# Down projection of a dequantised feed-forward layer: the fourth block of output columns goes from pre-scaled weights to integer weights with a running sum on VectorE

## The reference, cut to what matters

```python
x = x + tanh(g_xattn) * xattn(layernorm(x), ctx, ctx, ...)     # 32 batches, 64 channels, 512 columns
x = x + tanh(g_ffn) * ffn(layernorm(x), ...)

def dequant(qweight, scales, zeros):                # 4-bit words, groups of 128 rows
    return q * s[g] - (z[g] + 1) * s[g]             # = (q - (z + 1)) * s[g],  g = k // 128

def ffn(x2):                                        # x2: 2048 rows x 512
    gate, up = x2 @ Wg, x2 @ Wu                     # 512 -> 1376
    inter = gate * sigmoid(gate) * up
    return (inter @ Wd).astype(float16)             # 1376 -> 512, Wd dequantised
```

## Time and profile before

| what | value |
|---|---|
| median of three runs | 733.96 us |
| profiled execution, its own time | 733.95 us |
| its span, first to last instruction | 732.1 us |
| PE busy | 681.9 us (93%), 4995 matmuls |
| DVE busy | 585.6 us (80%), 774 instructions |
| ACT busy | 475.4 us (65%), 841 |
| POOL busy | 350.9 us (48%), 455 |
| mean granted TensorE clock | 0.991 |
| chain that ended last | PE 63%, DVE 10%, ACT 8%, issue 7%, POOL 5%, DMA 5% |

### The profile page before, as it was taken

One profiled execution on the slowest core, in us unless ns is written; L12 is line 12 of the kernel. 1 busy time (PEld: TensorE's weight loads), 2 busy tenths in 40 slices (PEclk: granted clock), 3 DMA queues, 4 the chain that ended last, 5 costly groups with the idle time before them and its releaser, 6 DMA issues.

```text
span 732.1 us, 14401 instructions
## 1 busy us (share of the span) xinstructions
PE 681.9 (93%) x4995; PEld 352.8 (48%) x4995; DVE 585.6 (80%) x774; ACT 475.4 (65%) x841; POOL 350.9 (48%) x455
## 2 busy tenths in 40 slices
PE   5789999999999999999999996999999999999995
PEld 4444554455455545545554542445444444454443
DVE  6567888888888888788888567889988888888885
ACT  4856786677668667767775746567655665665562
POOL 6312212222221322222234663788777867886783
PEclk9999999999999999999999999999999999999998
DMA  4112312330332122112200100000000001000101
GB/s 108 32 37 64 89 46 54 92 90 10 88 89 63 33 77 73 34 49 74 76 6 24 25 6 2 1 0 2 1 29 30 1 0 44 15 1 16 43 1 58
DMA packets 30509, 28.96 MB, mean 40 GB/s; under 512 B 20047, under 2 KB 20186, under 8 KB 30466
## 3 DMA queue, kind: packets, MB, share of 16 engines
q1 hardware_dynamic: 28058, 27.73, 14.0%
q10 hardware_dynamic: 2408, 0.70, 0.4%
HBM read 22.42 MB, written 4.23 MB: 36 GB/s over the span
## 4 chain that ended last, share of the span: by engine, by line
PE 63%; DVE 10%; ACT 8%; issue 7%; POOL 5%; DMA 5%; SPq 1%; DVEq 0%; ACTq 0%; POOLq 0%
PE small L1025 8%; PE small L996 7%; PE pair L982 6%; PE pair L1226 5%; PE pair L1227 4%; DVE acc L1529 4%; PE small L1012 4%; PE pair L1250 4%; DMA rn_rows<-rn_parts 3%; POOL rn_sq L433 3%; PE pair L961 3%; ACT eq L664 3%; PE pair L1262 3%; PE small L1062 3%; PE small L1226 2%
## 5 line engine op out<-in xcount | busy, mean ns | idle before, releaser
L1529 DVE SCALAR_TENSOR_TENSOR acc<-pair,scale_T,acc 128x512 f32<-128x512 f32 (+1 forms) x176 | 131.8, 749 | 27.2 <-ACT acc L782 14.7
L1442 DVE TENSOR_TENSOR eq<-eq,pair 128x1024 f32<-128x1024 f32 x64 | 78.1, 1221 | 54.0 <-PE pair L1079 53.9
L565 POOL TENSOR_TENSOR yT<-yT,y_scaled 128x512 f32<-128x512 f32 (+1 forms) x78 | 100.3, 1287 | 19.6 <-ACT y_scaled L813 18.6
L1226 PE MATMUL pair<-ek,w_gu 128*128 128x512 f16 (+1 forms) x235 | 91.8, 391 | 2.8 <-DVE acc L1529 1.8
L655 ACT ACTIVATE ek<-pair,kneg 128x512 f32<-128x512 f32 x128 | 86.7, 686 | 10.3 <-DVE kneg L1437 10.1
L1227 PE MATMUL pair<-ekT,w_gu 128*128 128x512 f16 (+1 forms) x235 | 89.5, 381 | 0.0
L1434 DVE TENSOR_REDUCE qmax<-pair 128x16 f32<-128x1024 f32 x64 | 77.7, 1214 | 8.1 <-PE pair L961 8.1
L1250 PE MATMUL pair<-in_hi,d_int 128*128 128x512 f32 (+1 forms) x132 | 73.4, 559 | 10.9 <-DVE yT L1572 10.8
L664 ACT ACTIVATE eq<-pair 128x1024 f32<-128x1024 f32 x64 | 65.6, 1025 | 22.6 <-PE pair L1101 22.3
L1437 DVE TENSOR_REDUCE kneg<-pair 128x2 f32<-128x1024 f32 x64 | 77.9, 1218 | 0.6 <-PE pair L982 0.2
L1529 DVE SCALAR_TENSOR_TENSOR acc<-small,scale_T,acc 128x512 f32<-128x512 f32 (+1 forms) x88 | 65.9, 749 | 13.1 <-ACT acc L782 6.5
(11 more groups left out here) (187 smaller groups left out, 1434.4 us busy)
## 6 DMA issues: line engine op xcount, KB each, us to landing
xall<-in_x SPq DMA_DIRECT2D x16, 256.0 KB, 2.6
ctx_raw<-in_ctx SPq DMA_DIRECT2D x16, 256.0 KB, 2.8
out_x<-xall SPq DMA_DIRECT2D x16, 256.0 KB, 2.0
zero<-zeros_plus SPq DMA_DIRECT2D x8, 344.0 KB, 5.5
packed<-in_L_ffn_gate_qweight SPq DMA_DIRECT2D x4, 688.0 KB
packed<-in_L_ffn_up_qweight SPq DMA_DIRECT2D x4, 688.0 KB
packed<-in_L_ffn_down_qweight SPq DMA_DIRECT2D x10, 256.0 KB
zero<-zeros_plus SPq DMA_DIRECT2D x5, 256.0 KB, 5.0
```

Of the source, the lines that this page charges most:

```text
L565: pool.tensor_tensor(yT16[:, nt, :] if it == IT - 1 else total, total, y_scaled[:, nt, :], ALU.add).then_inc(z_add, 1)
L1226: pe.matmul(gu_bank[count % 3][0:w, :], lhsT, xT_hi[:, g, rows], start=True, stop=False)
L1442: dve.tensor_tensor(e, e, dve_pair[:, :, :], ALU.mult).then_inc(q_norm, 1)
L1529: dve.scalar_tensor_tensor(out=acc[0:w, n % 2, m, :], in0=gu_bank[(8 * n + job) % 3][0:w, :], scalar=scale_T[0:w, it, 4 * m + g:4 * m + g ...
```

## The change

All four blocks of output columns use the integer weights `d_int`. Block 3 gets two matmuls per unit in a bank that is started anew for each unit, and a second sum on VectorE, `add_sum(n, 3)`, placed directly behind `add_sum(n, 2)`. TensorE's next `high_product` of block 3 waits for it. The semaphore `z_dve` now counts two per unit. `plain_scaled`, `plain_high`, `plain_low`, `plain_sum`, their tiles and the DMA for `d_scale` are gone. `rows_transposed` takes the blocks in the order 0, 2, 1, 3.

```diff
@@ sync @@
-            sp.dma_start(d_scale[:, :, :], matrices[2][1][:, PLAIN].partition_broadcast(P)).then_inc(d_scale_in, 16)
@@ gpsimd @@
             ffn_normalised(7)
-            plain_scaled()
@@ scalar @@
                     step(PAIRS + 1, PAIRS // 2, 1, False, False, True, drain=True)
-                    plain_high()
                     ffn_normalised(8)
                     ffn_normalised(9)
                 scaled(n - 2, 1)
-                if n > IT and n % IT == 1:
-                    plain_sum(n // IT - 1)
@@ tensor: high_product, low_product, rows_transposed @@
-                elif n and nt == 2:
-                    pe.wait_ge(z_dve, n)
+                elif n and nt >= 2:
+                    pe.wait_ge(z_dve, 2 * n + nt - 3)
...
-                elif it == 0 and j:
-                    pe.wait_ge(y_plain, j)
-                if nt == NJ - 1:
-                    if n == 0:
-                        pe.wait_ge(d_lo, 2)
-                    pe.matmul(z_bank[nt], wd_hi[0:w, it, :], in_hi[0:w, n % 2, :], start=it == 0, stop=False)
-                    pe.matmul(z_bank[nt], wd_lo[0:w, it, :], in_hi[0:w, n % 2, :], start=False, stop=False)
-                else:
-                    pe.matmul(z_bank[nt], d_int[0:w, it, nt * P:(nt + 1) * P], in_hi[0:w, n % 2, :], start=True, stop=False)
+                pe.matmul(z_bank[nt], d_int[0:w, it, nt * P:(nt + 1) * P], in_hi[0:w, n % 2, :], start=True, stop=False)
...
-                for nt in (0, 3, 2, 1):
+                for nt in (0, 2, 1, 3):
@@ vector: add_sum, the main loop and the end @@
                     if n:
-                        dve.wait_ge(z_dve, n)
+                        dve.wait_ge(z_dve, 2 * n + nt - 3)
...
-                if it == 1 and job == 4:
-                    plain_low()
...
                 add_sum(n - 3, 2)
+                add_sum(n - 3, 3)
...
             last_activated()
-            add_sum(UNITS - 3, 2)
-            add_sum(UNITS - 2, 2)
+            for n in (UNITS - 3, UNITS - 2):
+                add_sum(n, 2)
+                add_sum(n, 3)
             last_low_part()
-            for nt in (0, 2, 1):
+            for nt in (0, 2, 1, 3):
                 add_sum(UNITS - 1, nt)
```

More of the change, by code:

```diff
@@ L41 @@
 LATE_UNITS = (1, 4, 5, 7, 8, 9, 11, 12)
-PLAIN = slice((NJ - 1) * P, NJ * P)
 HEAD_MASKS, POOL_CONSTS = 13, 25
@@ L183, in layer @@
         acc = sb("acc", [P, 2, 2, CHUNK])
-        d_scale = sb("d_scale", [P, IT, P], F16)
         act_gate = sb("act_gate", [P, CHUNK])
@@ L187, in layer @@
         in_hi, in_lo = sb("in_hi", [P, 2, CHUNK], F32R), sb("in_lo", [P, 2, CHUNK], F32R)
-        wd_hi, wd_lo = sb("wd_hi", [P, IT, P], F32R), sb("wd_lo", [P, IT, P], F32R)
         ident16 = sb("ident16", [P, P], F16)
         y_scaled = sb("y_scaled", [P, 2, CHUNK])
-        yT = sb("yT", [P, NJ - 1, CHUNK])
+        yT = sb("yT", [P, NJ, CHUNK])
         yT16 = sb("yT16", [P, NJ, CHUNK], F16)
-        wd = sb("wd", [P, IT, P])
         zeros_plus = [nc.dram_tensor(f"zeros_plus{m}", shape, BF16, kind="Internal").ap()
@@ L238, in layer @@
             sem(n) for n in ("zwords_in", "zints_ready", "zplus_ready", "zplus_out"))
-        d_scale_in, tanh_ready = sem("d_scale_in"), sem("tanh_ready")
-        d_scaled, d_hi, d_lo, ident16_made = (sem(n) for n in ("d_scaled", "d_hi", "d_lo", "ident16_made"))
+        tanh_ready = sem("tanh_ready")
+        ident16_made = sem("ident16_made")
         gu_mm, s0_done, acc_done, gs_ready, inter_ready, in_hi_ready, in_lo_ready = (
             sem(n) for n in ("gu_mm", "s0_done", "acc_done", "gs_ready", "inter_ready", "in_hi_ready", "in_lo_ready"))
-        z_mm, z_act, z_dve, z_add, y_plain, yT_mm = (
-            sem(n) for n in ("z_mm", "z_act", "z_dve", "z_add", "y_plain", "yT_mm"))
+        z_mm, z_act, z_dve, z_add, yT_mm = (sem(n) for n in ("z_mm", "z_act", "z_dve", "z_add", "yT_mm"))
         out_ready, stored = sem("out_ready"), sem("stored")
@@ L274, in summed @@
         def summed(eng, n, nt):
-            if nt == 2:
-                eng.wait_ge(z_dve, n + 1)
+            if nt >= 2:
+                eng.wait_ge(z_dve, 2 * n + nt - 1)
             elif n % IT:
@@ L524, in ffn_normalised @@
                                    ALU.subtract, ALU.mult).then_inc(xn2_ready, 1)
[L526 to L533, removed]
             def activated(n):
@@ L797, in high_part @@
                 act.activation(in_hi[0:w, n % 2, :], inter[0:w, n % 2, :], ACT.Copy).then_inc(in_hi_ready, 1)
[L799 to L803, removed]
             def scaled(n, nt):
@@ L814, in scaled @@
                                scale=d_scale_T[:, nt, it:it + 1]).then_inc(z_act, 1)
[L816 to L821, removed]
             def ffn_normalised(k):
@@ L861, in _ @@
             scaled(UNITS - 2, 1)
-            plain_sum(CHUNKS - 1)
         @block.tensor
@@ L1257, in low_product @@
                     pe.wait_ge(in_lo_ready, n + 1)
[L1258 to L1263, removed]
+                pe.matmul(z_bank[nt], d_int[0:w, it, nt * P:(nt + 1) * P], in_lo[0:w, n % 2, :], start=False,
+                          stop=True).then_inc(z_mm, 1)
             def rows_transposed(j, t):
@@ L1273, in rows_transposed @@
                     pe.wait_ge(acc_done, 6 * UNITS)
-                for nt in (0, 3, 2, 1):
[L1275 to L1278, removed]
+                for nt in (0, 2, 1, 3):
+                    if t == 0 and j == CHUNKS - 1:
+                        pe.wait_ge(z_dve, 2 * UNITS - 1 + (0, 2, 1, 3)[nt])
                     elif t == 0:
@@ L1548, in last_low_part @@
                                   ALU.subtract).then_inc(in_lo_ready, 1)
[L1550 to L1555, removed]
             def add_sum(n, nt):
```

## The result

The changed kernel took 738.32 us (median of nine runs, 736.1 to 740.12), the kernel before 734.45 us in runs beside them (732.69 to 735.64). The ratio is 1.0049, 95% interval 1.0033 to 1.0064: slower by 2.4 to 4.7 us, 3.6 in the middle. Forecast was +4.85 us and 738.8 us: the time is 0.5 us under it, and the +4.85 lies just above that interval. The profiled execution took 737.31 us, its span is 735.3 us.

What follows compares the result with a forecast made beforehand. VectorE's in-order queue was taken to bound a plain unit at 6.06 us. Plain units +4.4, `fed_forward` units -0.2, `ffn_low` units +2.8, start -2.95, end +0.8 gave +4.85 us, so 738.8 us, range 736.3 to 741.9.

Steps and rivals of the forecast that it cites:

- The bound: Plain feed-forward units: VectorE's in-order queue sets 6.06 us; the 0.66 us sum less 0.46 us slack costs about +0.21 each.
- The three kinds of unit: Feed-forward units: 21 plain +4.4 us, twelve with `fed_forward` -0.2 us (6.72 each), five with `ffn_low` +2.8 us (6.66 each).
- Iterations 5 and 6: Feed-forward units where a5 of iteration 6 waits for a chain through GpSimd: both new sums hidden, 0 us.
- The start: Start of the feed-forward part: `plain_high` (1.36 us, ScalarE) and `plain_low` (1.60 us, VectorE) leave the path; -2.95 us taken.
- The end: Behind the last iteration: low products about 0.1 us later and four sums instead of three, +0.8 us.
- The first: Rival, plain and other units: TensorE sets the pace, a plain unit falls to 5.63 us, total 723.1 us; chance 0.06.
- The second: Rival, feed-forward units: a5's wait stays whole, the new sum comes on top, 17.8 us more, 756.6 us; chance 0.04.
- the fourth: Rival, feed-forward part: TensorE's clock falls because it stops three times a unit; four units add 19.4 us, 758.2; chance 0.03.
- The third: Rival, feed-forward start: no gain, as the norm's transfers or another queue end the wait at the old time; 741.8 us; chance 0.11.
- The rule that was weighed: VectorE's queue: a semaphore between two instructions costs nothing extra, so a unit needs 5.3 us of VectorE; the forecast went against it.
- the case worked out as 736.0: Variant of the forecast in which units with `ffn_low` hide the new sum too: 736.0 us, chance 0.03.

Runs made afterwards that it cites:

- `pe_more`: The changed kernel with the high product of block 3 done twice, giving TensorE its 44 matmuls back: 740.08 us, ratio 1.0083 to the kernel before.
- `half_sum`: The changed kernel with block 3's VectorE sum on 256 of 512 columns in nine of each chunk's eleven units: 729.43 us, ratio 0.9937 to the kernel before.
- again: The changed kernel run and profiled once more, unaltered, as base for the other runs: 737.48 us, ratio 1.0048 to the kernel before.
- the interleaved order: Gate and up jobs alternate, so successive VectorE adds write different tiles: changed kernel 713.46 us (ratio 0.9726), kernel before 722.92 us (0.9837).

## Why the prediction was right

**The bound.** Right. A busy share of 80 to 87% on VectorE hid that it had 0.46 us of slack per plain unit, and the sum needed 0.66. Measured 6.05 us against 6.06 forecast; `pe_more` and `half_sum` show both sides of it: 0.23 us more of TensorE cost the plain unit nothing, 0.27 us less of VectorE took 0.27 off.

**The three kinds of unit.** Each came within 0.01 us: 6.05, 6.71, 6.65. Iterations 5 and 6, held by GpSimd, hid both new sums (+0.01 to +0.04). Their total, +5.6 us against +6.8, is where the sum was too high. 0.7 us of that are two stops of VectorE of 0.35 us in the trace of before, in iterations 10 and 36, which I carried over and which neither profile of the changed kernel has. The rest is rounding: 0.195 instead of 0.21 in twenty units, -0.03 instead of -0.02 in twelve, 0.54 instead of 0.55 in four.

**The start.** The mechanism was right in both pieces, the size 0.37 us off: -2.58 for -2.95. The working had named the reason (TensorE's clock at the low level in iteration 1) and then taken the other end of its own range. The clock there was 0.57 again although TensorE's stop ahead of it had gone from 2.91 us to 1.56.

**The end.** Too small in the forecast: +1.0 with iteration 43, where +1.7 came. The profile of before had the low clock there too:

```profile
717.67:721.67 4.00, 3.21 (x9) 2.31 (x10) 1.69 (x4) 1.90 (x3) 1.04 (x1) 0.71 0.00 0
...
721.38 1.07 DVE L1547 TENSOR_TENSOR in_lo<-inter,in_hi 96x512 fp32r<-96x512 f32 x1
```

So its 21.42 us belong beside the 23.16 of the first profile after, and the +0.2 of again sets a full clock against a lowered one. The working put the second sum of unit 42, ahead of `last_low_part`, at 0.1 us. From the first sum behind iteration 43 to the last sums there are 5.69 us before (717.67 to 723.36) and 6.88 after (719.25 to 726.13), 1.2 us more. 0.57 of that is `in_lo` itself, 1.64 us for 1.07: before, it began when GpSimd's first addition had 0.52 us left, and after, 0.94 us later in this stretch, it met the second one with 1.09 left. The forecast had no term for that.

**The rivals.** The first, TensorE as the bound, is false here and holds for the plain units of the interleaved order, where one matmul less took 0.24 us off. The second (the wait of a5 stays) and the fourth (the clock falls in mid-stage) did not come: no idle of VectorE in a plain unit, clock 1.00 in 557 to 597. The third would have shown 24.4 us to the first sum.

**The rule that was weighed.** "VectorE: DVE Perf Modes" in the Trainium skill, section "The DRAIN you can't avoid", would have the semaphore free. In this kernel, by the two orders of the same six adds, a successor that waits for its neighbour on the same tile costs 0.19 us more, four times a unit; the measurement decides, though it leaves open whether the wait or the tile makes the price.

**In sum**, the bound, the slack and the price of the sum were right, and the closeness of the total is in part luck. With the same low clock at the end, the feed-forward part grew by 4.8 us between the two profiles (-2.6 + 5.6 + 1.7), beside +4.85 forecast; but the start was off by +0.4, the units by -1.2 and the end by +0.7, and these cancel. The medians give +3.6 (2.4 to 4.7), the second profile +3.2: less by what the end and single stops do in each execution, which the medians don't show one by one. A slip that changes nothing: the lower end of the range, 736.3, is said to be that of the case worked out as 736.0.

## What to carry to other kernels

When two engines pass work in a ring, don't ask which is busier. Add up the spacings of each engine's instructions over one period from their starts, those that follow on the same tile apart from those that don't, and compare each sum and each closed chain with the period: the price of one more instruction is its spacing less that engine's slack. Before work is moved onto an engine, look whether neighbours on it write the same tile; here reordering was worth six times what the change cost.

## What the runs showed of the hardware

- Two instructions of VectorE of 0.75 us with 512 columns start 0.66 to 0.68 us apart, and 0.85 apart when the second reads and writes the tile that the first wrote and waits for it.
- Halving an instruction's columns from 512 to 256 took 0.27 us off its spacing.
- TensorE's granted clock was 0.57 over 444 to 448 behind a stop of 1.56 us, with stops of 1.16 and 0.25 us shortly ahead of it. At the end, behind a stop of 2.1 us, it was 0.72 over 4 us in one execution of the changed kernel and 1.00 in another; TensorE's products there took 0.64 us longer in the first.
- In twelve profiles VectorE's last `in_lo` (`tensor_tensor`, 96x512, both inputs in SBUF) ended 0.55 us behind the end of the GpSimd addition that ran when it started: it took 0.80 us where that had 0.25 us left, 1.07 with 0.52, 1.47 with 0.91 and 1.64 with 1.09. A GpSimd addition that began while it ran took 1.72 to 1.74 us instead of 1.28.
